# Sums of squares for q's norm in float32 on TensorE, large buffers moved to multiples of 512 bytes, two small loads issued first

## What is computed

```python
def rmsnorm(x, g, eps=1e-5):
    var = jnp.mean(jnp.square(x), axis=-1, keepdims=True)
    return x * jax.lax.rsqrt(var + eps) * g

q = rmsnorm((layernorm(x) @ Wq).reshape(B, Sq, H, D), gq)
k = rmsnorm((ctx @ Wk).reshape(B, Skv, H, D), gk)
v = (ctx @ Wv).reshape(B, Skv, H, D)
attn = softmax(einsum('bqhd,bkhd->bhqk', q, k) / sqrt(D))
x = x + einsum('bhqk,bkhd->bqhd', attn, v).reshape(B, Sq, H * D) @ Wo
x = x + ffn(layernorm(x))     # gate, up, silu, rms norm, down
```

## Time and profile before

| | us |
|---|---|
| median of 3 runs (lowest, highest) | 479.24 (478.85, 480.3) |
| the profiled execution, its time | 480.16 |
| its span in the profile | 478.3 |
| busy PE / PEld | 415.7 / 317.7 |
| busy DVE / ACT / POOL | 430.5 / 430.7 / 387.9 |
| mean granted TensorE clock | 0.996 of full |

### The profile page before, as it was taken

The page is one execution under the profiler, slowest core; times in us unless marked ns, Lnnn a source line. Parts: engine busy times, 40 slices in busy tenths (PEclk is TensorE's granted clock), DMA queues, the critical chain, the costliest instruction groups (busy, mean ns, idle before and its releaser), DMA issues.

```text
span 478.3 us, 14736 instructions
## 1 busy us (share of the span) xinstructions
PE 415.7 (87%) x4554; PEld 317.7 (66%) x4554; DVE 430.5 (90%) x1249; ACT 430.7 (90%) x1454; POOL 387.9 (81%) x362
## 2 busy tenths in 40 slices
PE   0399866899999999999999999999999589788895
PEld 0288754677787777777777787777777355365563
DVE  2879899899999999999999999999998857999995
ACT  3379899999999999999999999999999569899993
POOL 2024958799999999999999999999998947888882
PEclk9999999999999999999999999999999989999999
DMA  7941734477465465555455465465666442001001
GB/s 270 427 183 24 287 65 83 61 114 144 89 118 100 88 119 100 96 111 101 89 113 105 92 117 98 90 119 99 98 103 108 94 78 34 1 33 35 22 33 58
DMA packets 140383, 50.20 MB, mean 105 GB/s; under 512 B 136000, under 2 KB 138048, under 8 KB 139456
## 3 DMA queue, kind: packets, MB, share of 16 engines
q1 hardware_dynamic: 139920, 48.78, 47.2%
q10 hardware_dynamic: 432, 1.05, 0.6%
HBM read 14.16 MB, written 2.10 MB: 34 GB/s over the span
## 4 chain that ended last, share of the span: by engine, by line
ACT 24%; issue 18%; POOL 17%; DVE 17%; DMA 10%; PE 9%; SPq 3%; ACTq 1%; POOLq 1%; DVEq 0%
ACT work L708 9%; DMA kT<-khl 8%; POOL rkq L553 5%; POOL phl L565 5%; PE SO L381 4%; ACT kjunk L746 3%; POOL work L543 3%; ACT qshl L730 3%; SPq L468 3%; ACT qhl L640 2%; ACT work L732 2%; DMA gqk<-in_gk 2%; PE KQ L381 2%; DVE ham L1245 2%; DVE qhl L1060 2%
## 5 line engine op out<-in xcount | busy, mean ns | idle before, releaser
L708 ACT ACTIVATE work<-SO,nbias,rkq 128x128 f32<-128x128 f32 x256 | 115.2, 477 | 6.0 <-DVE nbias L1083 4.5
L553 POOL TENSOR_TENSOR rkq<-kqe,negh 128x8 f32<-128x8 f32 x65 | 106.7, 1642 | 5.3 <-DVE kqe L1070 3.7
L381 PE MATMUL KQ<-hT,wqs 128*128 (+1 forms) x1536 | 99.4, 221 | 7.3 <-DVE wqs L932 6.7
L381 PEld LDWEIGHTS KQ<-hT,wqs 128*128 128x128 f16 x1536 | 92.0, 98 | 12.5 <-issue 10.0
L530 POOL TENSOR_TENSOR qshl<-work,qshl 128x512 f16<-128x512 f32 x64 | 74.5, 1163 | 27.1 <-ACT work L732 26.2
L381 PE MATMUL EB<-As,ohl 128*128 128x256 f16 x768 | 95.0, 274 | 0.4 <-issue 0.4
L381 PEld LDWEIGHTS EB<-As,ohl 128*128 128x128 f16 x768 | 75.5, 98 | 23.4 <-issue 1.4
L565 POOL TENSOR_TENSOR phl<-work,phl 128x512 f16<-128x512 f32 x64 | 74.0, 1156 | 19.7 <-DVE phl L1154 19.2
L381 PEld LDWEIGHTS SO<-kT,qhl 128*128 128x128 f16 x768 | 44.6, 98 | 37.0 <-DMA kT<-khl 22.4
L543 POOL TENSOR_TENSOR work<-work,rinv 128x512 f32<-128x512 f32 x64 | 66.6, 1040 | 3.0 <-DVE rinv L1028 2.9
L381 PE MATMUL SO<-kT,qhl 128*128 128x128 f16 x768 | 54.0, 220 | 12.1 <-DMA kT<-khl 8.0
(11 more groups left out here) (164 smaller groups left out, 930.5 us busy)
## 6 DMA issues: line engine op xcount, KB each, us to landing
xs<-in_xP SPq DMA_DIRECT2D x4, 512.0 KB, 22.2
stage<-in_wqP SPq DMA_DIRECT2D x4, 512.0 KB, 11.6
wvo<-in_woP SPq DMA_DIRECT2D x1, 2048.0 KB, 19.1
out<-wqs SPq DMA_DIRECT2D x16, 128.0 KB, 1.7
raw<-in_ctxT ACTq DMA_DIRECT2D x1, 1024.0 KB, 6.6
wvo<-in_wvP SPq DMA_DIRECT2D x1, 1024.0 KB, 14.7
raw<-in_ctxP SPq DMA_DIRECT2D x1, 1024.0 KB, 21.0
kT<-khl SPq DMA_TRANSPOSE x64, 3.1
```

The lines of the kernel that those rows point to most:

```text
L381: last = matmul(out, lhsT=left(i), rhs=right(j), start=start and n == 0, stop=stop and n == 2)
L553: pool.tensor_tensor(rkq[:, g % 4, :], kqe[:, g % 2, :], negh[:, 0:2 * HG], ALU.pow).then_inc(root_ok, 1)
L708: ins = act.activation(pe[:, s, c], SB[:, c], ACT.Exp, scale=rkq[:, (g - AT_X + 1) % 4, HG + h:HG + h + 1], bias=nbias[:, s, h:h + 1], acc ...
```

## The change

The squares are taken once, in float32, and TensorE multiplies them as float32 with a float32 column of ones. ACT's rounded square (730), POOL's difference (530), their semaphore and the buffer qshl (4096 bytes to a partition) are gone. `q_sums` issues 4 float32 products where it issued 8 float16 ones. st6 (384 bytes to a partition) is declared first, and khl, kT, qhl, phl, pT and ohl are declared right behind wvo. gq and gk are issued ahead of the context on ACT's queue.

```diff
+        st6 = sb("st6", [P, B, 6])
         xs = sb("xs", [P, B, DM])
...
+        khl = sb("khl", [P, 2, 2, GW], F16)
+        kT = sb("kT", [P, 2, 2, GW], F16)
+        qhl = sb("qhl", [P, 4, 2, GW], F16)
+        phl = sb("phl", [P, 2, 2, GW], F16)
+        pT = sb("pT", [P, 2, 2, GW], F16)
+        ohl = sb("ohl", [P, 2, 2, GW], F16)
         ident = sb("ident", [P, P], F16)
...
-        qshl = sb("qshl", [P, 2, 2, GW], F16)
...
-            def q_square_low(b, g):
-                if live(b, g, 0):
-                    s = g % 2
-                    need(pool, qsq_ok, b, g, 0)
-                    need(pool, ssq_ps, b, g, 0, 2)
-                    pool.tensor_tensor(qshl[:, s, 1, :], qsq[:, s, :], qshl[:, s, 0, :],
-                                       ALU.subtract).then_inc(qslo_ok, 1)
...
-            act.dma_start(cT_f, ctxT).then_inc(cT_in, 16)
             act.dma_start(gqk[:, 0:1], gq).then_inc(g_in, 16)
             act.dma_start(gqk[:, 1:2], gk).then_inc(g_in, 16)
+            act.dma_start(cT_f, ctxT).then_inc(cT_in, 16)
...
                     need(act, ssq_ps, b, g, 0, 2)
-                    act.activation(qshl[:, s, 0, :], QB, ACT.Square, scale=SQ_SHIFT)
-                    need(act, qslo_ok, b, g, 0, 2)
                     act.activation(qsq[:, s, :], QB, ACT.Square, scale=SQ_SHIFT).then_inc(qsq_ok, 1)
...
-                    need(te, qslo_ok, b, g, AT_SSQ)
+                    need(te, qsq_ok, b, g, AT_SSQ)
...
                     for h in range(HG):
-                        for a in range(2):
-                            ins = te.matmul(MB[:, h:h + 1], lhsT=qshl[:, s, a, h * P:(h + 1) * P],
-                                            rhs=ones[:, 0:1], start=a == 0, stop=a == 1)
+                        ins = te.matmul(MB[:, h:h + 1], lhsT=qsq[:, s, h * P:(h + 1) * P], rhs=ones_f[:, 0:1],
+                                        start=True, stop=True)
                     ins.then_inc(ssq_ps, 1)
```

More of the change, by code:

```diff
@@ L106, in build_program @@
         gqk = sb("gqk", [P, 2])
-        st6 = sb("st6", [P, B, 6])
         mv = sb("mv", [P, B, 2])
@@ L132, in build_program @@
         rkq = sb("rkq", [P, 4, 2 * HG])
-        khl = sb("khl", [P, 2, 2, GW], F16)
-        kT = sb("kT", [P, 2, 2, GW], F16)
-        qhl = sb("qhl", [P, 4, 2, GW], F16)
         qsq = work[:, 2 * GW:4 * GW].rearrange("p (s n) -> p s n", s=2)
-        qshl = sb("qshl", [P, 2, 2, GW], F16)
         smax_sb = sb("smax", [P, 2, HG])
@@ L144, in build_program @@
         pss = sb("pss", [P, 2, HG])
-        phl = sb("phl", [P, 2, 2, GW], F16)
-        pT = sb("pT", [P, 2, 2, GW], F16)
         hf = work[:, 0:XB * DM].rearrange("p (s n) -> p s n", s=XB)
@@ L155, in hf_of @@
             return hf[:, b % XB, :]
-        ohl = sb("ohl", [P, 2, 2, GW], F16)
         KQ = pb("KQ", [P, 2 * GW])
@@ L228, in build_program @@
         qsq_ok = sem("qsq_ok")
-        qslo_ok = sem("qslo_ok")
         ssq_ps = sem("ssq_ps")
@@ L569, in fill @@
                 A_root(b, g)
-                q_square_low(b, g)
                 c_lows(b, g)
```

## The result

The changed kernel takes 498.22 us (median of 6 runs, 495.59 to 499.7) against 479.34 us (6 runs, 478.85 to 480.3): ratio 1.0388, 95% interval 1.0358 to 1.0417. It is slower by 18.9 us; the forecast was 493.5, with 484 to 506 as the range. The profiled execution is the fastest of the six, 495.59 us with a span of 493.7, while the one of the kernel before, 480.16 us, lies near the upper end of its range.

A forecast was written before the change was run, and what follows sets the result against it. Four engines were nearly full, ACT most; after the change PE was to bound every loop step. 18.2 - 2.4 - 0.5 - 1.0 = +14.3 us on the profiled 480.16: 494.5, or 493.5 as a median; range 484 to 506.

The forecast's parts named there:

- slot: PE's time for the sums of squares in one step: 0.20 us before, 0.88 forecast, 0.68 more.
- The step: One loop step grows from 5.16 to 5.49 us with PE bounding; 0.33 us more, 18.2 over 55 steps.
- wait for kT: PE's wait ahead of the scores for kT's transpose to land, 0.29 us in the rows; should go.
- the loop over QB: From q product until buffer QB is free again: 5.24 us, 0.25 to spare; could stall PE if DVE is late.
- What is next behind PE: With nothing added on PE, DVE would bound the loop at 4.96 us a step, gaining at most 0.20.
- Rival (a): Faster: float32 passes under 0.07 us, slot stays 0.20, DVE bounds at 4.96; -15 us, 464.5; chance 0.09.
- The ends: Gains outside the steady loop: -2.4 up to the 8th group, -0.5 at the start, -1.0 behind the last group.
- of the 0.48 us on ACT I credit five steps, -2.4 us: Up to the 8th group PE has room, so ACT's freed rounded square counts in five steps: -2.4 us.
- The load order: At the start, gq and gk early let DVE's maximum of wq begin sooner: -0.5 us, bounds -1.7 to +0.9.
- Behind the last group: PE's 1.43 us wait for POOL's difference at the end goes; credited at -1.0 us.
- The addresses: Moving the buffers, transposes' included, changes nothing: 0, bounded by 0.1 us a step either way.
- PE's ring: Least time PE needs for one loop step in its fixed order: 4.81 us before, 5.49 forecast.

The follow-up runs named there:

- the float16 run: The changed kernel with its one square stored as float16 and multiplied by float16 ones, low halves left out, 4 passes instead of 8: 470.42 us, ratio 0.9808.

## Why the prediction was right

**The passes.** Forecast 8 passes, 0.11 us each, slot 0.88. Measured 0.86, 0.11 a pass, and 0.11 again for eight more. The two isolated products of the earlier trace rows were the right rows to lean on, although there was one of each.

**The step.** Forecast 5.49 us, measured 5.478; +18.2 us in the loop, measured +18.4. That PE would bound every step and its wait for kT would go, both hold between 110 and 320 us; the loop over QB that I feared didn't stall PE there (no row of PE waiting). Doubling the sums showed that each further 0.89 us in the slot is a further 0.89 us a step.

**What is next behind PE.** Forecast DVE at 4.96; the float16 run shows DVE the busiest at 4.92 to 5.02. Rival (a), a gain of 15 us, lost by its condition: no pass cost under 0.07 us. It was also too high. With 4 cheap passes and the new addresses the gain is 9 us, 7.8 of them in the loop ((5.162 - 5.020) x 55). Its sum has a slip: 480.16 - 14.9 is 465.3 us, 464.3 as a median, not 464.5.

**The ends.** Forecast -3.9 us in all, measured -3.0 in the profile (-0.9 ahead of the 8th group, -2.1 behind the 63rd). None of the three terms came out.

The largest, "of the 0.48 us on ACT I credit five steps, -2.4 us", gave nothing. From the first group's sums to the 8th's the kernel before takes 85.83 - 34.47 = 51.36 us and the changed one 84.93 - 33.43 = 51.50. With only the squares changed it is 51.21, and with one float16 square, where PE has less work than before, 51.17. The step that failed is "ACT bounds that stretch": in the same line of the earlier trace rows DVE is busy 28.81 of 30 us beside ACT's 29.82, and in the changed kernel DVE is still at 28.89 while ACT is at 29.03. A second engine as full as the first leaves a relief of the first without effect. That DVE's own order is what holds these steps is read from its busy time; no run made DVE lighter.

The load order was put at "-0.5 us", with the context landing "while ACT does the sum ahead of it". I had counted the two issues, 0.9 us, as the context's whole delay. It landed 4.7 us later (ACT begins it at 12.0 us), behind the slow stretch that the two small loads bring, and PE's first product slipped by 1.6 us, over the bound of +0.9. Alone, this edit costs 0.35% (0.21 to 0.49). That the profile of the changed kernel shows -1.0 us ahead of the first sums all the same is due to PE's early products at the higher rate (3.57 us for 32 instead of 5.39), which nobody forecast: luck, for this term.

Behind the last group I took -1.0 us for POOL's difference. From the 63rd group's sums to the 64th's the time fell from 6.08 to 4.14 us, by 1.9, so this term was half of what it should have been.

**The addresses.** Forecast 0, with 0.1 us a step as the bound. Measured alone 0.087 us a step, within the bound, and hidden under PE's ring as forecast: with and without them the kernel with float32 squares (context first) takes 496.77 and 496.15 us, which these runs can't tell apart. The reason I gave was poor. I compared two sources that were both off a boundary and concluded from 3.1 and 3.2 us that the remainder doesn't matter; no row of before had an aligned one.

**The total.** 494.5 us forecast for the profiled execution, 495.6 measured; 493.5 for the median, 498.2 measured. The loop's 18.4 us carry the forecast, and they are understood. That the total of the profiled execution came within 1.1 us is in part luck: it is the fastest of six runs. By the medians the kernel is 18.9 us slower, which leaves the ends a gain of 0.5 us instead of 3.9 if the loop is the same in every run, as it is in the profiles. The changed kernel's runs spread over 4 us, those of the kernel before over 1.5, and I had carried the distance of 0.92 over.

## What to carry to other kernels

Before moving work between engines, add up each engine's ring, the time of one step's work from start to start in its own timeline; here PE had 0.35 us a step to spare, and float32 stationary operands against one moving column added 0.66 to the 0.20 of the float16 ones. A float32 pass costs nearly the same with one moving column (0.86 / 8 = 0.108 us) as with 128 (3.57 / 32 = 0.112), so a float32 product that only sums columns is dear for what it does: keep float16 there, or fewer passes. Before crediting an engine's relief, look whether a second engine is as full in the same stretch. Put what a DMA transpose reads on a multiple of 512 bytes (it cost nothing and gave 1%), and look at what stands behind a small load on the same queue before moving it ahead.

## What was not expected of the hardware

Two loads of 128 values of 4 bytes, issued ahead of 1 MB on their queue, moved its landing from about 7.3 us to 12.0 (0.9 of it is its later issue), and the rate of all DMA fell from 387 to 199 GB/s between 4 and 6 us, while x, on the other queue, landed earlier: DVE began its statistics at 5.35 instead of 6.99 us.

A DMA transpose lands 0.3 to 0.5 us earlier with its source on a multiple of 512 bytes; 64 bytes off loses all of it, and the destination 64 bytes off loses nothing.

With PE busy without a break, exponentials on ACT had shorter records (457 ns mean against 477, their accumulator reads 203 against 222). Why stays open.
